# Column tiles of a two-layer convolution: layer 0's matmuls split into two of 64 rows by 32 columns, layer 1's left at 64 by 64

## The reference

```
# layer 0: w2d depends on the image, by an angle from its normalized mean
x = x + conv3x3(group_norm(x), w2d[image])      # zero padding
# layer 1: the same weights for every image, written there as an FFT product
x = x + circular_conv3x3(group_norm(x), weight)
```

## Time and profile before

| | |
|---|---|
| median of 2 runs | 1730.03 us (1729.79 to 1730.26) |
| the profiled execution's own time | 1728.56 us |
| its span, first to last instruction | 1726.8 us |
| PE busy | 1630.3 us, 94% |
| DVE, ACT busy | 1294.9 and 1144.3 us |
| mean granted TensorE clock | 0.99 of 2.4 GHz |

### The profile page before, as it was taken

How to read it: one execution, slowest core, us unless ns; L and a number is a source line. 1 busy time by engine, 2 the same in 40 slices (tenths; PEclk the granted TensorE clock), 3 DMA queues, 4 the chain that set the end, 5 groups by cost and what they waited for, 6 DMA issues and landing times.

```text
span 1726.8 us, 63815 instructions
## 1 busy us (share of the span) xinstructions
PE 1630.3 (94%) x28906; PEld 1260.8 (73%) x28906; DVE 1294.9 (75%) x1744; ACT 1144.3 (66%) x1029; POOL 112.0 (6%) x347
## 2 busy tenths in 40 slices
PE   5888888789899999999999999999999999999999
PEld 4787778655467777887688778867786778677766
DVE  5999899889977777777777777777777777777600
ACT  6888878589666666666666666666666666666444
POOL 0000000031100020002000200020002000100100
PEclk9999999989999999999999999999999999999999
DMA  9999999935466566666666666666666665665255
GB/s 386 421 421 422 422 422 421 379 92 161 119 199 211 201 198 211 210 201 198 213 207 201 198 212 208 200 199 211 210 200 198 209 212 185 213 206 204 112 203 203
DMA packets 99668, 409.99 MB, mean 237 GB/s; under 512 B 16883, under 2 KB 17384, under 8 KB 83048
## 3 DMA queue, kind: packets, MB, share of 16 engines
q1 hardware_dynamic: 98025, 405.94, 65.7%
q0 software_dynamic: 672, 0.08, 0.1%
q10 hardware_dynamic: 735, 0.37, 0.1%
HBM read 271.83 MB, written 134.50 MB: 235 GB/s over the span
## 4 chain that ended last, share of the span: by engine, by line
PE 75%; DVE 12%; issue 7%; ACT 4%; DMA 2%; DVEq 0%; ACTq 0%; SPq 0%; POOL 0%; POOLq 0%
PE ps L527 72%; DVE x L810 9%; ACT x L633 2%; DMA x<-x_pix 1%; ACT x L668 1%; ACT x L670 1%; DMA x<-wf 1%; DVE x L1013 1%; DVE x L864 1%; DVE stats L1030 1%; PE ps L452 1%; PE ps L453 0%; ACT x L674 0%; PE ps L456 0%; PE ps L463 0%
## 5 line engine op out<-in xcount | busy, mean ns | idle before, releaser
L527 PE MATMUL ps<-x,wc 64*64 64x512 f16 x24540 | 1339.9, 377 | 10.3 <-DVE x L1013 9.4
L527 PEld LDWEIGHTS ps<-x,wc 64*64 64x64 f16 x24540 | 992.7, 107 | 351.5 <-issue 21.4
L864 DVE SCALAR_TENSOR_TENSOR x<-xin,gnp,x 128x1028 f16<-128x1028 f32 x247 | 320.3, 1298 | 234.6 <-ACT x L633 234.5
L633 ACT ACTIVATE x<-xin,gnp 128x1028 f16<-128x1028 f32 x247 | 286.4, 1160 | 307.6 <-PE ps L527 302.4
L684 ACT ACTIVATE outb<-ps,bias 128x1024 f32<-128x1024 f32 x256 | 285.3, 1114 | 155.0 <-PE ps L527 155.0
L1013 DVE SCALAR_TENSOR_TENSOR x<-ps,gnp,x 128x1024 f16<-128x1024 f32 x256 | 325.1, 1270 | 24.3 <-ACT x L670 24.0
L452 PE MATMUL ps<-x 128*128 128x129 f16 x2048 | 254.1, 224 | 59.0 <-DVE x L810 58.6
L810 DVE SCALAR_TENSOR_TENSOR x<-x 128x2048 bf16<-128x2048 f32 x128 | 282.8, 2283 | 19.3 <-DMA x<-wf 17.4
L1030 DVE BATCH_NORM_STATS2 stats<-ps 128x6 f32<-128x512 f32 x440 | 283.6, 687 | 11.1 <-ACT x L674 8.5
L619 ACT ACTIVATE x<-x 128x2048 f16<-128x2048 f32 x128 | 240.1, 1908 | 52.6 <-PE ps L453 36.0
L452 PEld LDWEIGHTS ps<-x 128*128 128x128 f16 x2048 | 197.7, 98 | 78.6 <-DVE x L810 78.6
(11 more groups left out here) (144 smaller groups left out, 292.2 us busy)
## 6 DMA issues: line engine op xcount, KB each, us to landing
x<-x_pix SPq DMA_DIRECT2D x128, 1024.0 KB, 11.5
out<-outb SPq DMA_DIRECT2D x256, 512.0 KB, 3.7
xin<-x_tiles SPq DMA_DIRECT2D x239, 514.0 KB, 3.6
xin<-x_tiles SPq DMA_DIRECT2D x8, 642.5 KB, 4.1
x<-x_tiles SPq DMA_DIRECT2D x9, 514.0 KB, 7.2
w<-taps_scratch SPq DMA_DIRECT2D x60, 8.0 KB, 2.7
w<-taps_scratch SPq DMA_DIRECT2D x30, 16.0 KB, 3.1
taps_scratch<-x POOLq DMA_DIRECT2D x21, 3.0 KB, 1.8
```

Of the source, the lines that this page charges most:

```text
L527: return nc.tensor.matmul(to.rearrange("p (r w) -> p r w", w=NCOL), lhs, two, start=first, stop=last)
L633: nc.scalar.activation(planes[:, 0, a:a + w], x_at(g), ACT.Identity, scale=gnp[:, 1, b:b + 1]).then_inc(hi0_ready, 1)
L864: V.scalar_tensor_tensor(planes[:, 1, a:a + w], x_at(g), gnp[:, 1, b:b + 1], planes[:, 0, a:a + w], ALU.mult, ALU.subtract).then_inc(lo0_r ...
```

## The change

Each matmul of layer 0 becomes two: one for the first 32 of its 64 output channels and one for the other 32, with the same moving data and the matching half of the weights. Layer 1 goes on as before. `tile_columns` gives the pieces, and the loop over `kind` gets a loop over them. The waits, the semaphores raised (by the last piece), and the order of jobs, steps, halves and kinds stay.

```diff
+            def tile_columns(layer, kind):
+
+                return [(64 * kind, 32), (64 * kind + 32, 32)] if layer == 0 else [(64 * kind, 64)]
+
-            def quarter(layer, i, n, job, k, half, kind, q, first, last):
+            def quarter(layer, i, n, job, k, half, kind, lane, width, q, first, last):
...
-                lhs = (wc0 if layer == 0 else wc1)[rows, (i // NCH) % 2, whl, kind, dj, :]
+                lhs = (wc0 if layer == 0 else wc1)[rows, (i // NCH) % 2, whl, kind, dj, lane - 64 * kind:lane - 64 * kind + width]
...
-                to = ps[64 * kind:64 * kind + 64, bank, :]
+                to = ps[lane:lane + width, bank, :]
...
                     for kind in range(2):
-                        done = quarter(layer, i, chunk_of(job), job, k, half, kind, q, half == 0 and k == 0,
-                                       half == 1 and k == len(PASSES) - 1)
+                        for lane, width in tile_columns(layer, kind):
+                            done = quarter(layer, i, chunk_of(job), job, k, half, kind, lane, width, q,
+                                           half == 0 and k == 0, half == 1 and k == len(PASSES) - 1)
```

## The result

| | before | after |
|---|---|---|
| median | 1730.03 us | 5625.58 us (5618.0 to 5633.16, 2 runs) |
| profiled execution, its span | 1728.56, 1726.8 us | 5618.0, 5616.2 us |
| ratio | | 3.25 (95% interval 3.233 to 3.271) |
| mean granted TensorE clock | 0.99 | 0.549 |

Slower, as forecast, but by 3890 us in the profiled executions where 1778 were expected, and far above the range's end of 3850 us. The page of the changed kernel says where to look: engines' busy shares, and, in the 40 slices of the span, PE's busy tenths and its granted clock.

A forecast was written before the change was run, and what follows sets the result against it. The prediction took PE as the bound, at 216 ns a step. To 1728.6 us it added 857 us of streams in series and 921 us of changes, 1778 together, making 3507 us (median 3508); range 3120 to 3850 us.

The forecast's parts named there:

- mixed steps: 3969 steps where one half is in layer 0 and the other in layer 1; expected to stream twice 216 ns.
- The streams in series: In mixed steps the two sizes stream one after the other, 3969 x 216 ns = 857 us.
- A and B: A: four 64x32 matmuls, one half, layer 0; B: two 64x64, one half, layer 1; some 321 and 331 ns.
- Rivals 1 and 2: Size belongs to the tile: 1730 us, chance 0.07; only overlapping tiles wait, at layer seams: 1826 us, chance 0.04.
- rival 3: No emptying, but the rate of instructions binds in layer 0 and mixed steps: 2391 us; chance 0.02.
- The price of a change: At each of 8373 size changes the array empties and a load shows: 110 ns each, 921 us.
- Steps all in layer 0: 1080 steps with both halves in layer 0, sixteen instructions in 216 ns: taken at 0, upper end 233 us.
- PE's first run up to the first `means`: Sign at the kernel's start: should last as before; if longer, the instructions' rate has a price.
- 26 ns a pair: Pace in the earlier trace; 8 x 26 = 208 ns, just under 216, so layer 0 steps cost nothing.
- rival 4: The clock falls to 1.2 GHz in mixed steps, doubling streams (another 1715 us) and changes (921): over 6100 us; chance 0.03.

The follow-up runs named there:

- e2_by_step: The step-wise kernel: the changed kernel with tile size alternating from step to step, for both halves and both layers alike; 2475.99 us.
- the threes with burst: Changed kernel with three steps of half 0, then three of half 1, and 40 full-array matmuls behind each `means`; 3027.77 us.
- e1_all32: Changed kernel with both layers in tiles of 64 by 32; 1986.79 us, ratio 1.146.
- e5_one_half: Changed kernel with all tiles 64 by 64 and both halves on partitions 0 to 63, leaving out products of 64 to 127; 5452.87 us.
- e11_half_burst: e5_one_half with 40 full-array matmuls added behind each `means`; 3108.58 us.
- e10_burst: Changed kernel with 40 full-array matmuls added behind each `means`; 5647.72 us.
- pairs: Changed kernel with the halves' order turned round in every other step, so groups of one size stand in pairs; 4605.86 us.
- the threes: Changed kernel with three steps of half 0, then three of half 1; 3524.88 us, run again 4687.13 and 4109.32 us.
- e3_blocks64: Changed kernel with all tiles 64 by 64, half 0 taking six steps, then half 1 six; 1761.38 us.
- e6_pieces: Changed kernel with all tiles 64 by 64 and every matmul in two of 256 elements; 1976.83 us, ratio 1.144.

## Why the prediction was wrong

The forecast's mechanism is what happens, but the step that failed is the clock: the prediction put a fall of it at nothing in its sum, and PE kept the full clock for only 17 us of mixed steps. That is some 2030 of the 3890 us.

**The streams in series: right.** A and B never stream side by side (loads at 479.00, 479.32, 479.66, a group each 0.33 us). Rivals 1 and 2, by which sizes belong to tiles, are refuted by the same rows, and so is rival 3: a mixed step takes 0.66 us and not 0.324.

**The price of a change: nearly right.** 110 ns were taken. The Trainium skill's rule that a change of mode drains TensorE (TensorEngine Tiling (Array Packing), "Key Properties") holds for 64x64 and 64x32. Measured, from one execution each: 121 ns by the step-wise kernel; and by the threes with burst, 3027.8 - 1729.6 - 8 x 8.5 (bursts) - 857 (series) = 373 us for its 3087 changes, 121 ns again. Groups take 0.33 us where 321 and 331 ns were worked out. Had the clock held, the changed kernel would have come to 1729 + 857 + 8373 x 0.121 = 3599 us, 2.6% above the forecast and inside its range. That is worked out, not run.

**Steps all in layer 0 at no cost: nearly right.** By the prediction's own sign, PE's first run up to the first `means`, the number of instructions has a price: the `means` came 5.6 us later, with 10.8 us of waits for "issue". It is small here because PE had waited 8.7 us for DVE there before. The reason given, 26 ns a pair from sixteen small pairs, spoke of a short stretch and not of a lasting supply, which fails at that pace (all-32, 257 us).

**The clock: the step that failed.** It is rival 4, given 0.03. Its price, over 6100 us, took a change to double with the clock too; it only went from 121 to 130 ns, and without that second 921 us it comes to 5220, with the single-size steps of the alternating part that it left out (1323 x 0.211 = 279 us) to 5500. So the rival was right in kind, and without these two errors its size would have been within 2.2% of the time. The excess of 3890 us splits so: 857 series, 1013 changes at full clock, and for the clock 7938 + 1323 streams x 0.211 = 1954 and some 75 us of changes; the sum is 3899, and the first 35 jobs add some 6.

What misled was the earlier trace rows. They show 1002 matmuls of the whole array in 74 us keeping the clock, with pauses; I carried this over to a half-used array without a row for it. The runs part the two: emptying with the whole array keeps the clock for 2 ms (`e2_by_step`), half the array without emptying keeps it until a break (`e5_one_half`) and all through if a full burst follows each break (`e11_half_burst`), and half the array with emptying behind each single group doesn't keep it even with bursts (`e10_burst`). So between two breaks neither alone loses the clock; both together, with an emptying behind every group, lose it within 17 us, while pairs and threes of groups keep it up to a break, as half the array alone does. Half the array can lose it at a break even without emptying, and doesn't regain it; the whole array with emptying fell behind its first `means` too and was back 3.4 us later. Whether these are two causes, or one measure of how much of the array works over time, the runs don't tell apart. The trace of before could not show this: it has half the array only for the first 9 steps.

**The range.** I left a gap out of it on purpose, down to the rivals near 1730, and stopped at 3850 above; rival 4 lay beyond that end with 0.03. The clock has two levels and every stream doubles with it, so a range that trusts one level is narrow by a factor, not by per cents.

What stays open: why one `means` drops the clock and another of the same program doesn't. In the four profiles that lost it late the fall came 3 to 4 us behind a `means`, but in the alternating part the threes passed four such places in one run and none in another. Each kernel with a burst ran once. The breaks were followed by bursts, not taken away, so the break's own part is inferred from where the falls stand and from what the burst prevents.

## What to carry to other kernels

Do not mix tile sizes on TensorE in neighbouring instructions: each change empties the array (0.12 us here) and whatever would have streamed beside it stands in series. Blocks of one size cut the number of changes (from 8373 to 3087 in the threes), but in no kernel here what stands in series. For a PE-bound kernel, ask of every reordering what part of the array is in use and whether it pauses, and price the answer at both clock levels; a mean granted clock in the page is read before anything else. A half-used array may hold the clock for hundreds of us and lose it behind a break of 1.4 us with tiny matmuls, so a single run of such a kernel says little; a burst of full-array matmuls behind the pause may pay for itself many times.

## What the runs showed that I had not expected

- Adding 68 us of useless matmuls took a kernel from 5453 to 3109 us.
- Once down, the clock stayed down under continuous half-array streams for 4.9 ms (`e5_one_half`), the same streams that held it up for 2.5 ms (`e11_half_burst`).
- Within one tile size PE starts matmuls of free tiles ahead of waiting ones that stand six steps before them: 222 ns a step against 360 in program order (`e3_blocks64`).
- PE can run out of instructions: with 16 in 216 ns it waited 226 and 193 times, for 195 and 159 us (`e1_all32`, `e6_pieces`).
